# Gated block with ternary weights, one core: one store for the last tile, bias and weight loads issued earlier, three small products moved from VectorE to ScalarE

## The reference

```python
# stage 1: one of four experts per row, chosen by the row's token id
h = layernorm(x)
y = silu(h @ ctx[e].T) * (h @ ctx[e].T) @ ctx[e].T   # e = min(token // 6250, 3)
x1 = x + tanh(g_xattn) * y
# stage 2: a feed-forward block with quantized activations and ternary weights
def bit_linear(x, w, b):
    s = 127 / clip(max|x| over the row, 1e-5)
    x_dq = clip(round(x * s), -128, 127) / s
    gamma = clip(mean|w|, 1e-5)
    w_dq = clip(round(w / gamma), -1, 1) * gamma
    return x_dq @ w_dq.T + b
h = layernorm(x1)
out = x1 + tanh(g_ffn) * bit_linear(silu(bit_linear(h, gate)) * bit_linear(h, val), out_w)
```

## Time and profile before

| | us |
|---|---|
| median of 3 runs | 309.68 (309.02 to 309.77) |
| the profiled execution | 310.04 |
| its span in the trace | 308.3 |
| TensorE busy | 291.8 (95% of the span) |
| VectorE busy | 261.4 (85%) |
| ScalarE busy | 219.2 (71%) |
| GpSimd busy | 238.5 (77%) |
| granted TensorE clock | 0.998 of full speed |

### The profile page before, as it was taken

The page is one execution under the profiler, slowest core; times in us unless marked ns, Lnnn a source line. Parts: engine busy times, 40 slices in busy tenths (PEclk is TensorE's granted clock), DMA queues, the critical chain, the costliest instruction groups (busy, mean ns, idle before and its releaser), DMA issues.

```text
span 308.3 us, 5341 instructions
## 1 busy us (share of the span) xinstructions
PE 291.8 (95%) x1438; PEld 141.0 (46%) x1439; DVE 261.4 (85%) x496; ACT 219.2 (71%) x276; POOL 238.5 (77%) x261
## 2 busy tenths in 40 slices
PE   1989999999999999999889999999999999999994
PEld 1445555544444555444334444444444444444453
DVE  5899987787988968679998999999998899888982
ACT  4959686777887746677986796668866876675650
POOL 5656854788888979936678799998989887977863
PEclk9999999999999999999999999999999999999999
DMA  6685798759997873923043635764445423543142
GB/s 261 228 314 202 271 313 305 251 120 307 336 279 189 230 218 102 292 60 109 19 92 72 121 69 119 122 151 88 107 115 119 85 68 86 119 87 82 54 102 105
DMA packets 58902, 49.10 MB, mean 159 GB/s; under 512 B 51135, under 2 KB 51135, under 8 KB 56576
## 3 DMA queue, kind: packets, MB, share of 16 engines
q1 hardware_dynamic: 54304, 35.43, 45.1%
q0 software_dynamic: 4576, 13.40, 12.5%
HBM read 28.35 MB, written 10.00 MB: 124 GB/s over the span
## 4 chain that ended last, share of the span: by engine, by line
PE 83%; DVE 7%; DMA 3%; issue 2%; POOL 2%; ACT 2%; DVEq 0%; POOLq 0%
PE banks L632 27%; PE banks L705 17%; PE banks L726 17%; PE banks L714 16%; PE banks L639 2%; DMA raw<-raw 2%; PE banks L609 1%; DMA xg<-in_x,gather_at 1%; DVE turned L1053 1%; DVE raw L1207 1%; DVE raw L1202 1%; POOL w_both L476 1%; DVE gu_sb L1102 1%; POOL out L548 1%; PE banks L745 1%
## 5 line engine op out<-in xcount | busy, mean ns | idle before, releaser
L476 POOL TENSOR_TENSOR w_both<-raw 128x1024 f32<-128x1024 f32 (+1 forms) x32 | 74.9, 2342 | 7.7 <-DVE raw L1202 6.8
L632 PE MATMUL banks<-w_both,turned 128*128 x348 | 80.0, 379 | 0.6 <-ACT turned L861 0.5
L939 ACT ACTIVATE w_both<-w_both,magic,raw 128x1024 f32 (+1 forms) x31 | 38.2, 1234 | 35.5 <-DVE raw L1221 35.5
L705 PE MATMUL banks<-tern,raw 128*128 128x512 bf16 x256 | 60.5, 379 | 1.6 <-DMA raw<-raw 1.2
L714 PE MATMUL banks<-tern,raw 128*128 128x512 bf16 x256 | 60.5, 379 | 1.3 <-DVE raw L1194 1.3
L726 PE MATMUL banks<-tern,xg 128*128 128x512 bf16 x240 | 56.1, 379 | 0.7 <-DVE raw L1230 0.7
L632 PEld LDWEIGHTS banks<-w_both,turned 128*128 128x128 f16 x348 | 34.0, 98 | 37.5 <-issue 2.3
L1194 DVE SCALAR_TENSOR_TENSOR raw<-banks,raw 128x1024 f32<-128x1024 f32 x32 | 40.8, 1276 | 4.7 <-issue 4.5
L1202 DVE SCALAR_TENSOR_TENSOR raw<-banks,raw 128x1024 f32<-128x1024 f32 x32 | 40.9, 1278 | 3.6 <-PE banks L714 3.6
L1207 DVE TENSOR_REDUCE raw<-w_both 128x1 f32<-128x1024 f32 x32 | 38.8, 1212 | 3.1 <-POOL w_both L476 2.9
L705 PEld LDWEIGHTS banks<-tern,raw 128*128 (+1 forms) x256 | 24.9, 98 | 32.1 <-DMA raw<-raw 1.4
(11 more groups left out here) (134 smaller groups left out, 420.2 us busy)
## 6 DMA issues: line engine op xcount, KB each, us to landing
raw<-in_ctx SPq DMA_DIRECT2D x4, 1024.0 KB, 6.7
raw<-in_L_ffn_gate_w SPq DMA_DIRECT2D x4, 1024.0 KB, 6.8
raw<-in_L_ffn_val_w SPq DMA_DIRECT2D x4, 1024.0 KB, 7.5
raw<-in_L_ffn_out_w SPq DMA_DIRECT2D x4, 1024.0 KB, 6.1
raw<-x_low SPq DMA_DIRECT2D x8, 257.5 KB, 3.5
raw<-x_high SPq DMA_DIRECT2D x8, 257.5 KB, 3.4
raw<-in_L_ffn_gate_b SPq DMA_DIRECT2D x1, 1024.0 KB, 5.4
raw<-in_L_ffn_val_b SPq DMA_DIRECT2D x1, 1024.0 KB, 9.5
```

The lines of the kernel that those rows point to most:

```text
L476: nc.gpsimd.tensor_tensor(z[:, t % 2, 2 * D * c:2 * D * c + width], g_sb[:, c, 0:width], v_sb[:, c, 0:width], ALU.mult).then_inc(z_made, 1)
L632: last = nc.tensor.matmul(acc[:, :], a[:, k * P:(k + 1) * P], flat(w[:, bass.ds(e4 + k, 1), :]), start=(k == 0 and i == 0), stop=(k == KD ...
L705: last = nc.tensor.matmul(ring[pair][:, b, :], flat(xiT[:, bass.ds(t % 2, 1), k, :]), tern[:, k * HC + 2 * c + b, :], start=(k == 0), stop ...
L939: nc.scalar.activation(zq[:, a:b], flat(z[:, bass.ds(t % 2, 1), a:b]), ACT.Identity, scale=flat(sc[:, bass.ds(t, 1), 12:13]), bias=magic[: ...
```

## The change

The last tile is stored by one indirect DMA after both halves are added. The three bias loads wait for 12 signs instead of 16. VectorE's two products of the x scale and the weight scales (L1183, L1184) become one ScalarE instruction with two columns, and its product for the output scale (L1222) becomes a ScalarE instruction. The floor 1e-5 is kept in an extra column behind z, written once by GpSimd, which the second `z_max` reads too; `z_max_both` then takes maximum and division in one instruction. SyncE issues out_w's piece 8 right behind piece 7, piece 9 after the gather of unit 10, piece 10 after the transpose of unit 9, piece 11 after that of unit 11.

```diff
@@ sync
+            load_weights(8)
+            gathers_landed(10)
+            load_weights(9)
             for i, j in enumerate(H_DMA[:-2]):
                 turn_h(j)
-                if 8 + i < 12:
-                    load_weights(8 + i)
+                if i in (0, 2):
+                    load_weights(10 + i // 2)
...
-            sp.wait_ge(signed, G)
+            sp.wait_ge(signed, bias_frees)
...
             for n in range(YS):
-                sp.wait_ge(stored[n], 16 * ((TILES - 2 - n) // YS + 1))
-            for n in range(2):
-                sp.wait_ge(stored_last[n], 16)
+                sp.wait_ge(stored[n], 16 * TILES // YS)
@@ gpsimd
                     pool.wait_ge(y_done, UNITS)
+                    nc.gpsimd.memset(z[:, :, H:H + 1], 1e-5).then_inc(z_floor, 1)
                     z_pair(0, 0)
...
-                pool.wait_ge(o_made, t + 1)
+                pool.wait_ge(o_made, t + 2 if t == TILES - 1 else t + 1)
...
-            for t in range(TILES - 4, TILES - 1):
+            for t in range(TILES - 4, TILES):
                 store(t)
-            for c in range(2):
-                store_last(c)
@@ scalar
                 nc.scalar.activation(xq, xn, ACT.Identity, scale=flat(sc[:, bass.ds(t, 1), 2:3]),
                                      bias=magic[:, 0:1]).then_inc(xq_made, 1)
+                nc.scalar.activation(flat(sc[:, bass.ds(t, 1), 3:5]), gam[:, 0:2], ACT.Copy,
+                                     scale=flat(sc[:, bass.ds(t, 1), 1:2])).then_inc(xs2_made, 1)
...
+            def out_scale(t):
+                act.wait_ge(zs_made, t + 1)
+                nc.scalar.activation(flat(sc[:, bass.ds(t, 1), 13:14]), flat(sc[:, bass.ds(t, 1), 11:12]), ACT.Copy,
+                                     scale=out_gam[:, 0:1]).then_inc(zs2_made, 1)
...
                     z_round(t - 1, 1, start)
+                    out_scale(t - 1)
@@ vector
                 v.reciprocal(col(t, 2), col(t, 1)).then_inc(xs_made, 1)
-                v.tensor_scalar(col(t, 3), gam[:, 0:1], col(t, 1), None, ALU.mult).then_inc(xs2_made, 1)
-                v.tensor_scalar(col(t, 4), gam[:, 1:2], col(t, 1), None, ALU.mult).then_inc(xs2_made, 1)
...
-                v.tensor_reduce(col(t, 5 + c), z[:, t % 2, 2 * D * c:2 * D * (c + 1)], AX.X, ALU.max,
+                if t == 0 and c == 1:
+                    dve.wait_ge(z_floor, 1)
+                v.tensor_reduce(col(t, 5 + c), z[:, t % 2, 2 * D * c:2 * D * (c + 1) + c], AX.X, ALU.max,
...
-                v.tensor_scalar(col(t, 9), col(t, 5), col(t, 6), 1e-5, ALU.max, ALU.max).then_inc(z_step, 1)
-            def z_gamma(t):
-                dve.wait_ge(z_step, 2 * t + 1)
-                v.tensor_scalar(col(t, 11), col(t, 9), 1 / QMAX, None, ALU.mult).then_inc(z_step, 1)
+                v.tensor_scalar(col(t, 11), col(t, 5), col(t, 6), 1 / QMAX, ALU.max, ALU.mult).then_inc(z_step, 1)
...
                 v.reciprocal(col(t, 12), col(t, 11)).then_inc(zs_made, 1)
-                v.tensor_scalar(col(t, 13), col(t, 11), out_gam[:, 0:1], None, ALU.mult).then_inc(zs2_made, 1)
...
-            row = x1_in[:, t % XR, TOKEN:ROW].bitcast(u32)
-            for c in range(2):
-                last = v.tensor_scalar(half_row[:, c:c + 1], row, 2.0, float(c), ALU.mult, ALU.add)
-            last.then_inc(last_named, 1)
```

More of the change, by code:

```diff
@@ L31, in gated_block @@
     XR = 11
+    ZROW = H + 8
     EARLY = 8
@@ L48, in gated_block @@
     out_rows = out.rearrange("b s d -> (b s) d")
-    out_halves = out.rearrange("b s (c d) -> (b s c) d", c=2)
     tok_v = token_ids.rearrange("b (q c) -> (b q) c", c=COLS)
@@ L107, in gated_block @@
         one = sb("one", [P, 1], f32)
-        half_row = sb("half_row", [P, 2], u32)
         scratch = tern[:, 2 * G:2 * G + 4, :].rearrange("p g d -> p (g d)").bitcast(f32)
@@ L154, in gated_block @@
         x1_in = area(-(-XR * ROW // 8) * 8)[:, 0:XR * ROW].rearrange("p (b d) -> p b d", b=XR)
-        x_frees = 6
+        x_frees, bias_frees = 6, 12
         bias_g, bias_v, bias_o = area(H), area(H), area(D)
@@ L162, in gated_block @@
         area = areas_of(w_both[:, :])
-        z = area(2 * H).rearrange("p (b d) -> p b d", b=2)
+        z = area(2 * ZROW).rearrange("p (b d) -> p b d", b=2)
         zq = area(H)
@@ L233, in gated_block @@
         xs2_made, zs2_made, outgam_made, bias_scaled = sem("xs2_made"), sem("zs2_made"), sem("outgam_made"), sem("bias_scaled")
+        z_floor = sem("z_floor")
         z_turned_ps, z_turned_last = ([sem(f"{name}{half}") for half in range(2)] for name in ("z_turned_ps", "z_turned_last"))
@@ L236, in gated_block @@
         o_done, o_made, biased, stored = sem("o_done"), sem("o_made"), sem("biased"), [sem(f"stored{n}") for n in range(YS)]
-        o_last, last_named, stored_last = sem("o_last"), sem("last_named"), [sem(f"stored_last{n}") for n in range(2)]
+        o_last = sem("o_last")
         block = ctx.enter_context(nc.Block(no_gpsimd_drain=True))
@@ L542, in store @@
                     in_=x1_in[:, t % XR, 0:D], in_offset=None).then_inc(stored[t % YS], 16)
[L544 to L550, removed]
             for t in range(TILES):
@@ L1000, in _ @@
             z_round(0, 1, start=True)
+            out_scale(0)
             with act.Fori(2, TILES - 3) as t:
@@ L1009, in _ @@
             nc.scalar.activation(zi_last[:, 0:H // 2], zq[:, 0:H // 2], ACT.Identity, bias=magic[:, 1:2]).then_inc(zi_made[0], 1)
+            out_scale(TILES - 1)
             act.wait_ge(z_turned_ps[0], 1)
@@ L1189, in pre_gate @@
                 if c == 0:
-                    dve.wait_ge(xs2_made, 2 * (t + 1))
+                    dve.wait_ge(xs2_made, t + 1)
                 dve.wait_ge(g_done, n + 1)
@@ L1212, in z_max_both @@
                 dve.wait_ge(zmax_made, 2 * t + 2)
-                v.tensor_scalar(col(t, 9), col(t, 5), col(t, 6), 1e-5, ALU.max, ALU.max).then_inc(z_step, 1)
-            def z_gamma(t):
-                dve.wait_ge(z_step, 2 * t + 1)
-                v.tensor_scalar(col(t, 11), col(t, 9), 1 / QMAX, None, ALU.mult).then_inc(z_step, 1)
+                v.tensor_scalar(col(t, 11), col(t, 5), col(t, 6), 1 / QMAX, ALU.max, ALU.mult).then_inc(z_step, 1)
             def z_scales(t):
-                dve.wait_ge(z_step, 2 * t + 2)
+                dve.wait_ge(z_step, t + 1)
                 v.reciprocal(col(t, 12), col(t, 11)).then_inc(zs_made, 1)
-                v.tensor_scalar(col(t, 13), col(t, 11), out_gam[:, 0:1], None, ALU.mult).then_inc(zs2_made, 1)
             def finish(t):
@@ L1296, in _ @@
                     z_max_both(t - 1)
-                    z_gamma(t - 1)
                 if 2 <= t < TILES - 2:
@@ L1327, in _ @@
             z_max_both(t)
-            z_gamma(t)
             z_scales(t)
```

## The result

| | before | after |
|---|---|---|
| median, us (20 runs each) | 309.97 (309.02 to 314.24) | 308.87 (306.92 to 310.02) |
| ratio after/before | | 0.9946, 95% interval 0.9927 to 0.9965 |
| profiled execution, us | 310.04 | 307.41 |
| its span, us | 308.3 | 305.7 |

The change makes the kernel faster by 0.54%, about 1.7 us at the ratio; the two medians of the table lie 1.10 us apart. The forecast was 2.44 us. The profiled execution gained 2.6 us, more than the typical one; the runs after spread over 3.1 us. Every ratio in this document leaves out runs more than 1.5% above the fastest of the same kernel, such as the one of 314.24 us.

What follows compares the result with a forecast made beforehand. VectorE was taken to pace stage 2's first tiles, TensorE to be full from 183 us. 310.04 - 1.37 - 1.17 + 0 + 0.1 = 307.60; with the runs' median 0.36 lower, forecast 307.2 us, range 306.0 to 308.9.

Steps and rivals of the forecast that it cites:

- What bounds the kernel: TensorE is full from 183 to 298 us; before that, VectorE sets the pace of stage 2's first tiles.
- Biases, 1.37 us: Bias loads 9.8 us sooner free the transpose of tile 0; TensorE's first gate gains 1.20 us, plus 0.17 without a restart.
- VectorE's small work, 1.17 us: 0.58 us saved per VectorE slot shrinks TensorE's stalls in stage 2's first tiles, 2.54 - 1.37 = 1.17 us.
- ScalarE's two instructions, 0.1 us each: Two added ScalarE instructions per slot lengthen its crowded run at 147 to 156 us, ahead of silu of tile 2.
- The out weights, net 0: Earlier out-weight loads delay the transpose of unit 9, TensorE losing about 1.2 us near 74, later regained; bounds -0.7 and +1.2.
- absorb the delay by unit 13: TensorE's later waits for gu, about 0.35 us each with restarts, take up the 1.2 us lost near 74 us.
- The end, +0.1 us: One last store instead of two halves starts 0.3 us after the last addition and lands 3.0 us later: 0.1 us slower.
- Slower: piece 9 holds the transpose of unit 9: Rival: piece 9, issued just before that transpose, makes it take 8 us, landing near 74; 310.6 us, chance 0.05.
- the analogous gather cost 7.6: Argument against the slower rival: the gather of 43.0 us, with two pieces beside it, took 7.6 us.
- Biases alone: Rival: GpSimd's late z_pair makes VectorE wait and eats VectorE's savings, so only the biases count; 308.4 us, chance 0.14.

Runs made afterwards that it cites:

- the biases alone: Kernel before with only the three bias loads issued at the twelfth sign instead of the sixteenth: 309.52 us, ratio 0.9961.
- the slower profile of the changed kernel: Profiled execution of the unmodified changed kernel when timed again beside two variants: 309.12 us; that set's median 309.36 us, ratio 0.9957 to the kernel before.
- the weights alone: Kernel before with only the out-weight loads moved to the changed kernel's order: 312.34 us, ratio 1.004.
- the pair of experiments: Changed kernel with the old out-weight order, once with one last store (308.05 us, 0.9909), once with the two half stores (308.48 us, 0.9932).
- the products alone: Kernel before with only the scale products on ScalarE and the z floor in the maximum: 309.29 us, ratio 0.9958.

## Why the prediction was right, and the step that failed

**Right**: faster, and the median 308.87 inside the range 306.0 to 308.9, by 0.03 us. That was luck in part: ten of the twenty runs lie above 308.9, and the upper bound had been set for the rival in which the biases alone count. The gain is 1.7 us by the ratio and 1.10 us by the medians, instead of 2.44.

- **What bounds the kernel.** TensorE full from 183 us on, VectorE's pace before: as read.
- **Biases, 1.37 us.** The loads went out at 110.07 us (forecast 109.9), the transpose landed without a wait, the first gate started at 130.45 (forecast 130.33) and the group behind at -1.31. Measured 1.31 by the trace, 1.2 by the ratio of the biases alone (interval 0.4 to 2.0). VectorE's wait for them is gone as well.
- **VectorE's small work, 1.17 us.** The course by tile was forecast as -1.88, -2.25, -2.54 and came as -1.79, -2.01, -2.44, so 1.13 us beyond the biases; alone, the ratio gives 1.3. The 0.24 us by which -2.01 falls short of -2.25 are VectorE's own: 0.09 of them stand already at -1.79, most of it because the queue started from -1.31 and not -1.36 and the x products saved 0.20 and not 0.22; then, in VectorE's timelines, from the end of `z_max` (156.29 before, 154.51 after) to the end of the second pre_gate (158.75 and 156.75) it took 2.46 us and takes 2.24, so that 0.22 us are saved where I had 0.36. The last stall shrank from 0.7 to 0.2 where I had 0.35, and that made up for it. That z_pair of tile 2 then holds VectorE showed as the 0.88 us wait at 157.68 us, and TensorE had the slack for it.
- **ScalarE's two instructions, 0.1 us each.** Together they cost ScalarE 0.25 us, near the 0.2 of the sum, but not as two equal halves: 0.06 for the x products, which fall into the time that `x_unshift` waited for `x_round` anyway, and 0.19 for the output product, at a place where the queue had not been waiting. The estimate from the Trainium skill (VectorE: DVE Perf Modes, The TRN2 errata), 0.19 us each with no overlap, agrees with the 0.19 and 0.18 us between starts; for the x products it is three times what they add. The silu of tile 2 starts at 154.11 instead of 155.49, 1.38 us sooner where I had 1.5. ScalarE stands nowhere in the chain of work that ends with the second pre_gate of tile 2, so its two instructions take nothing from the -2.01.
- **The out weights, net 0.** This is the step that failed. The text had the order right (piece 9 out near 62.6, in front of the transpose of unit 9; its own numbers, 55.4 + 7.6, give 63.0) and its price near 74 us too: 1.2 us estimated, 1.19 measured in the slower profile of the changed kernel. What failed is "absorb the delay by unit 13": 1.05 of 1.19 us was left at 112 us, 2.42 of 3.56 with the weights alone. The waits for gu that were to absorb it are too small: TensorE's list of waits of the kernel before names 0.5 us in all between 64 and 119 us. The second thing missed: I took one landing time, 7.6 us, for the gather of unit 10, while piece 9's issue hangs on it; in the traces of kernels with this wait it lands between 61.2 and 64.1 us, and where piece 9 went out from 63.5 us on, the transpose took 5.7 to 7.1 us. The term measured +1.1 to +1.2 us by ratios (0.9946 and 0.9957 against 0.9909 and 0.9922; 1.0040 alone), at its upper bound of +1.2. The trace's other terms are 1.31 + 1.13 + 0.17 = 2.6 us, the gain of the first profiled execution; less 1.1 for this one, that leaves 1.5 us, near the 1.7 of the ratio.
- **The end, +0.1 us.** It came as -0.17 in the changed kernel's profile (3.55 us from the last addition to the end, 3.72 before) and -0.2 in the pair of experiments. The store went out 0.27 us behind the addition (forecast 0.3), and landed in 2.7 us (3.0 in the sum).

**The rivals.** "Slower: piece 9 holds the transpose of unit 9" had a chance of 0.05 and was the mechanism, at a smaller size: it happened in its own form in the kernel with the weights alone (gather 7.8 us, landing 73.07, just past the 73 us from which it was to decide). In the changed kernel it costs 1.1 us by the ratios, and the gain of the other parts stays larger. The argument against it, that the analogous gather cost 7.6, carried nothing: the two executions that wait for the gather alone and pay have 7.8 and 7.9. The rule of the Trainium skill (DMA: Bandwidth & Descriptors, Queues, rings and completion order), that descriptors of one issuing engine are consumed in ring order, fits the table above: where piece 9 was still 4 us or more from its landing when the transpose was issued, the transpose landed only behind it, and where it had been issued 12 us before and was 0.6 us from its landing, the transpose took its 3.2 us. What no run here separates is that order from plain sharing of the engines. "Biases alone" lies nearest the median by number (308.4), but its mechanism is refuted by the products alone, 0.9958, and by the stalls that went. The sum of two measured gains and one measured loss gave nearly the same time.

## What to carry to other kernels

A load moved earlier can be paid by the transfer that it is now put in front of: write down, for each queue, what stands behind the moved issue and when the load will have landed, and read the profile of more than one execution, since a wait on another queue's landing makes that distance vary. Where two pieces can go out without a wait, long before the transfer that someone waits for, that is safer than an issue keyed to a third transfer. Small work moved from the busiest engine can cost the other one its whole advance of the queue (0.19 us here) or next to nothing (0.06 us, where it falls into a wait for the instruction before): look at what stands behind the place where you put it.

## What the runs showed that I had not expected

- A transpose of 3.2 us took 5.7 to 7.1 us with a 1 MB load issued 2.2 to 1.0 us ahead of it in the same queue, and landed 1.0 to 1.2 us behind that load.
- TensorE's granted clock stayed 1.00 in the executions with waits of 0.42 and 1.08 us near 72 us, and fell to an average of 0.72 over 72 to 78 us behind the wait of 1.84 us; that fall cost 1.7 us, nearly as much again as the wait. The length of the wait does not decide it by itself: in the same execution the clock stayed at 1.00 behind an equally long wait at 132.8 us. In the profile of the products alone, a wait of 2.28 us ahead of 133.61 us was followed by 0.50 over 134 to 137 us, so part of what makes that execution the slowest of its twelve is the clock.
- A ScalarE instruction on one or two columns is 0.28 to 0.29 us long by the profile, and the next one starts 0.18 to 0.19 us after it; the 0.195 us of the smallest one in the earlier trace rows was no upper bound for duration.
